# Attention in 11 parts per group of heads in place of 16, their transposes two parts behind, and two outputs earlier in the last group

## The chip, the cores and the metric

One core of a Trainium2 chip runs the kernel. A core has TensorE (PE, matmuls and transposes), VectorE (DVE), ScalarE (ACT) and GpSimd (POOL), which run their own instruction streams and wait for one another by semaphores; SyncE (SP) issues most DMAs. The metric is the time of one execution in microseconds: 1339.72 us, the median of 3 runs (1336.94 to 1344.49). The profile is of one further execution.

## The reference, cut to what matters

Four sequences of 512 tokens (width 256) go through a latent-attention layer, a mixture of experts, a state-space layer and a gated feed-forward layer. Only the attention is touched:

```python
q = rmsnorm(x @ w_qa, q_norm_w) @ w_qb            # 16 heads, 128 plain + 64 rotary columns
kv = rmsnorm(kv_c, kv_norm_w) @ w_kvb             # 64 latent columns, one rotary key for all heads
scores = jnp.einsum('blhd,bmhd->bhlm', q, k) * scale
scores = jnp.where(mask[None, None], scores, -1e30)        # causal
attn = jax.nn.softmax(scores, axis=-1)
out = jnp.einsum('blhm,bmhd->blhd', attn, v).reshape(B, L, H * DV) @ w_o
```

Everything is computed in float32 here; the causal mask is added by a small bf16 matmul.

## The kernel before, in words

**Rows and groups.** The attention takes one sequence at a time, called a row here (`b` from 0 to 3), and in it four groups of four heads (`hg` 0 to 3; `g` counts the 16 groups over all rows). The weights are folded so that a head's query is a 64-wide latent with a 64-wide rotary part, and its key and value are the shared latents: `QT` holds the turned queries of a group (two buffers), `KT` the keys, `V` the values.

**Parts.** A group is cut into `NU` = 16 parts `u` (one slot each), a tile of 128 queries `i = u // 4` by a head `h = u % 4`. Because of the causal mask part `u` has `(i + 1) * 128` score columns: 128 for the first four parts, then 256, 384 and 512. A part goes through: `scores` on PE (a float32 product, two matmul instructions, and the mask, L615 and L616) into one of three banks; `maximum` on DVE (L1001); `exps` on ACT (L829, which also gives the row sum); `inverse_sum` on DVE (L1006); `normalize` on DVE, in place in `prob` (L1012); `transposes` on PE, one per 128 columns, into one of two banks (L624); `evacuate` on DVE to the buffers `prob01`, `prob2`, `prob3` (L1021, L1024). Then `values` multiplies whole query tiles by `V` (L641; n = 0 takes tiles 0 and 1, n = 1 tile 2, n = 2 tile 3), and ACT copies the result to `OT` (`take_values`, L841). `output` (L712) multiplies a tile of `OT` by the folded output weights, eight products of 256 columns, and DVE adds it to `x` (`residual`, L950).

**The order of work** is written out by hand, per engine and slot `at`; an engine does its list in order. PE's slot: scores of part `at`; work for the next group's queries, if its slot says so (`rope_product` L542 and L546, `latent_product` L555 and L560, `rope_transposes` L567; in a row's last group the next row's `project`, L510); transposes of part `at - LAG`, with `LAG` = 3 (the last three parts of a group fall in the next group's first slots); values; routing products. DVE's slot: maximum of `at`, inverse sum of `at - 1`, evacuation of `at - LAG`, normalisation of `at - 1`, then a step of the routing of the row before (`route_slot`: the choice of six experts per token, L1226 to L1306). ACT's slot: the exponential of `at`, then copies (L795, L803, L809, L841). POOL turns queries (`rope`, L1125 to L1129) and sends the row before to the experts' buffer (`send`, L1375).

The slots of the extra work are in tables: `ROPES_AT` {1, 4}, `LATENTS_AT` 7, `TURN_AT` {11, 14}, `PROJECT_AT` {5, 9}, `VALUES_AT` {12: 0, 16: 1, 20: 2}, where a slot of 16 or more is `at - 16` in the next group. Semaphore counts keep the order: `exps` of part u needs the transposes of u - 4 (four `prob` buffers), scores of u the exponential of u - 3, transposes of u the evacuation of u - 2.

**Row ends.** After a row's last group the last transposes and values run, then the four outputs, mixed with the start of the next row. In row 3 outputs 0 and 1 stand in slots 14 and 15 of the last group; then values 1, the last transposes, values 2, a transposed half of the layer norm (L393), output 2, routing logits (L1183) and output 3. After that the shared expert (L1646 to L1665) runs beside the routing and sending of row 3, and then the experts' loop.

Of the kernel before, what the change touches and what calls it, by code (L numbers as in the profile page):

```python
# [15 lines left out]
P = 128  # L16
# [9 lines left out]
HG = 4  # L26
# [29 lines left out]
def build(nc, a, out):  # L56

    ctx = ExitStack()
    with ctx:
# [432 lines left out]
        def output_bank(b, i):  # L492
            return bank[(QUERY[0], QUERY[1], 4, 5)[i] if b == BATCH - 1 else 4 + i % 2]
# [7 lines left out]
        def att_tensor(pe):  # L501
# [48 lines left out]
            def latent_product(g, at):  # L550

                hg = g % GROUPS
                for p in range(2):
                    h = hg * HG + 2 * p
                    nc.tensor.matmul(bank[at[p]][:], wl1[:, h:h + 2, :].rearrange("p h c -> p (h c)"), cq1,  # L555
                                     start=True, stop=False)
                for c in range(0, SEQ, 2 * P):
                    for p in range(2):
                        r = slice(QL2 * p, QL2 * (p + 1))
                        last = nc.tensor.matmul(bank[at[p]][:, c:c + 2 * P], wl2[r, hg, :], cq2[r, c:c + 2 * P],  # L560
                                                start=False, stop=c + 2 * P == SEQ)
                last.then_inc(A["q"], 1)
# [23 lines left out]
            def first_latents(b):  # L586
                g = GROUPS * b
                pe.wait_ge(A["qs"], QSTEPS * g + 2)
                latent_product(g, (6, 7))
# [14 lines left out]
            def scores(g, u):  # L604
                i, h = u // HG, u % HG
                n = (i + 1) * P
# [3 lines left out]
                if h == 0 and i % 2 == 0:  # L610
                    pe.wait_ge(A["qte"], 2 * g + i // 2 + 1)
                if u == 0 and g % GROUPS == 0:
                    pe.wait_ge(A["kr"], g // GROUPS + 1)
                at = score_bank(g, u)
                nc.tensor.matmul(at[:, 0:n], QT[g % 2][:, h, i * P:(i + 1) * P], KT[:, 0:n], start=True, stop=False)  # L615
                nc.tensor.matmul(at[:, i * P:n], identb[:], futureb[:], start=False, stop=True)\  # L616
                    .then_inc(A["s"], 1)

            def transposes(g, u):
                i = u // HG  # L620
                pe.wait_ge(A["norm"], NU * g + u + 1)
                need(pe, A["pte"], NU * g + u - 1)
                for j in range(i + 1):
                    last = nc.tensor.transpose(bank[TRANS[u % 2]][:, j * P:(j + 1) * P],  # L624
                                               prob[:, u % 4, j * P:(j + 1) * P], ident)
                last.then_inc(A["pt"], 1)

            def values(g, n):
                tiles = VALUE_TILES[n]
                pe.wait_ge(A["pte"], NU * g + HG * (tiles[-1] + 1))  # L630
# [16 lines left out]
            def slot(g, at, with_next):  # L647
# [4 lines left out]
                elif not with_next:  # L652
# [1899 lines left out]
```

## Time and profile before

| | |
|---|---|
| median of 3 runs | 1339.72 us |
| the profiled execution's own time | 1341.87 us |
| its span, first to last instruction | 1340.0 us |
| mean granted clock of PE | 0.961 of full speed |
| busy in the span: PE, DVE, ACT, POOL | 90%, 61%, 36%, 28% |
| attention, from the first scores to the end of the last output | 59.5 to 638.2 us |
| the rest: before, and from there to the end | 59.5 us, 701.8 us |

The span is that of the profiled execution alone, and is compared with that execution's own time, not with the median. A share of busy time is an average over the whole program: PE's 90% doesn't say that PE sets the pace in each part of it. Where one engine waits for another is read from the stretches, the chain of waits and the timeline. Busy times of PE are modelled to each matmul's end and overlap; the time that a matmul takes of PE is the distance to the next one's start, which is what the chain of waits lists.

### The profile page before, as it was taken

The page shows a single profiled execution, that of the slowest core. Times are in us where ns is not written, and L with a number is a line of the kernel's source. Part 1 is how long each engine was busy: PE and PEld are TensorE (multiplying, and loading weights), DVE is VectorE, ACT ScalarE, POOL GpSimd, SP SyncE. Part 2 cuts the span into 40 slices and gives each one's busy share as a digit, 9 for nine tenths or more (in the row PEclk, how much of TensorE's full clock was granted, in tenths as well). Part 3 has the DMA queues.
Part 4 walks back from the last instruction along what each step waited for, and adds up shares of the span by engine and source line. Part 5 has one row for each costly group of instructions (what it writes and reads, how often), then busy time and mean ns, then how long its engine had stood idle before and what let it go on. Part 6 is the DMA issues. An engine that isn't in the chain of part 4 may idle for free.

```text
span 1340.0 us, 19647 instructions
## 1 busy us (share of the span) xinstructions
PE 1212.5 (90%) x6073; PEld 760.7 (57%) x6073; DVE 822.7 (61%) x2243; ACT 487.3 (36%) x1124; POOL 374.5 (28%) x462
## 2 busy tenths in 40 slices
PE   6899999999998899988979999998777959999988
PEld 3566566555655466555547777775434436465454
DVE  6477877788688777785433334336684655676431
ACT  2456435552555435552301111111522513525311
POOL 0242023251425423352520000213781450401200
PEclk9799999999999999999989999999888988999989
DMA  9999999999900100010458888872220020000000
GB/s 330 412 420 419 420 421 420 420 419 418 418 23 33 64 1 1 6 58 34 136 139 255 272 268 287 269 246 79 71 68 27 24 71 16 24 7 10 0 16 16
DMA packets 86624, 235.76 MB, mean 176 GB/s; under 512 B 9712, under 2 KB 20624, under 8 KB 86288
## 3 DMA queue, kind: packets, MB, share of 16 engines
q1 hardware_dynamic: 68112, 192.80, 38.8%
q0 software_dynamic: 9216, 25.18, 5.9%
q10 hardware_dynamic: 9216, 16.78, 3.3%
q8 instruction: 42, 0.69, 0.2%
q14 instruction: 38, 0.31, 0.1%
HBM read 66.96 MB, written 167.77 MB: 175 GB/s over the span
## 4 chain that ended last, share of the span: by engine, by line
PE 66%; DVE 21%; issue 5%; ACT 2%; another core or an unknown queue 2%; SPq 2%; DMA 1%; POOL 1%; ACTq 0%; POOLq 0%; DVEq 0%
PE bank L615 6%; PE bank L641 4%; PE bank L1505 4%; PE bank L624 4%; PE bank L1527 4%; PE bank L1766 3%; PE bank L1772 3%; DVE r L1012 3%; DVE negmax L1001 3%; PE bank L712 3%; PE bank L1783 3%; PE bank L542 2%; PE bank L1927 2%; PE bank L1490 2%
## 5 line engine op out<-in xcount | busy, mean ns | idle before, releaser
L829 ACT ACTIVATE r<-bank,negmax 128x128 f32<-128x128 f32 (+3 forms) x256 | 135.2, 528 | 179.7 <-DVE negmax L1001 172.3
L615 PE MATMUL bank<-r 128*128 128x512 f32 (+3 forms) x512 | 185.8, 446 | 2.9 <-ACT r L809 2.9
L1001 DVE TENSOR_REDUCE negmax<-bank 128x1 f32<-128x128 f32 (+3 forms) x256 | 123.9, 485 | 49.5 <-PE bank L616 37.0
L624 PE MATMUL bank<-tables,r 128*128 128x128 f32 x640 | 118.3, 284 | 24.8 <-DVE r L1012 22.5
L1125 POOL TENSOR_TENSOR r<-r,tables 128x256 f32<-128x256 f32 x56 | 40.9, 731 | 338.4 <-ACT r L795 333.0
L1375 POOL DMA_INDIRECT sent<-r,slots x96 | 93.6, 975 | 102.1 <-ACT r L829 52.2
L624 PEld LDWEIGHTS bank<-tables,r 128*128 128x128 f32 x640 | 70.3, 142 | 87.2 <-DVE r L1012 49.7
L1614 DVE COPY r<-bank 128x512 f32<-128x512 f32 x64 | 41.2, 686 | 116.2 <-PE bank L1536 75.0
L1012 DVE TENSOR_SCALAR r<-r,rrow 128x128 f32<-128x128 f32 (+3 forms) x256 | 112.1, 438 | 0.3
L615 PEld LDWEIGHTS bank<-r 128*128 128x128 f32 x512 | 79.2, 194 | 21.4 <-issue 16.8
L1021 DVE COPY late<-bank 128x256 f32<-128x256 f32 (+1 forms) x128 | 60.8, 475 | 29.5 <-PE bank L624 24.4
L1392 POOL DMA_INDIRECT r<-sent,slots x16 | 15.2, 953 | 213.2 <-DMA sent<-r 209.5
L1728 POOL TENSOR_TENSOR r<-tables,r 128x1024 f32<-128x1024 f32 x16 | 31.2, 1963 | 155.1 <-DVE r L2147 126.9
L1572 ACT ACTIVATE r<-bank 128x512 f32<-128x512 f32 x32 | 19.1, 598 | 145.8 <-PE bank L1505 138.6
L712 PE MATMUL bank<-spent,r 128*128 128x256 f32 x256 | 59.9, 390 | 3.9 <-ACT r L841 3.9
L1505 PE MATMUL bank<-r 128*128 128x256 f32 x256 | 62.5, 388 | 0.0
L1527 PE MATMUL bank<-r 128*128 128x256 f32 x256 | 61.3, 382 | 0.0
L712 PEld LDWEIGHTS bank<-spent,r 128*128 128x128 f32 x256 | 48.8, 195 | 14.2 <-ACT r L841 5.5
L1606 DVE COPY r<-bank 128x512 f32<-128x512 f32 x64 | 41.3, 684 | 24.4 <-PE bank L1490 22.4
L616 PE MATMUL bank<-futureb,identb 128*128 128x128 bf16 x256 | 56.2, 220 | 0.0
L1527 PEld LDWEIGHTS bank<-r 128*128 128x128 f32 x256 | 48.0, 190 | 8.9 <-issue 2.7
L1021 DVE COPY w2buf<-bank 128x512 f32<-128x512 f32 x64 | 43.2, 678 | 14.0 <-PE bank L624 14.0
(289 smaller groups left out, 2449.4 us busy)
## 6 DMA issues: line engine op xcount, KB each, us to landing
sent<-gath SPq DMA_DIRECT2D x8, 16384.0 KB, 93.7
r<-waT_dram SPq DMA_DIRECT2D x64, 304.0 KB, 3.1
r<-sent SPq DMA_DIRECT2D x64, 256.0 KB, 3.9
sent<-r ACTq DMA_DIRECT2D x64, 256.0 KB
w2buf<-wcT_dram SPq DMA_DIRECT2D x64, 48.0 KB, 3.2
r<-w_o_dram SPq DMA_DIRECT2D x1, 2048.0 KB, 22.5
sent<-gath SPq DMA_DIRECT2D x2, 1024.0 KB, 60.6
out_dram<-x SPq DMA_DIRECT2D x4, 512.0 KB, 2.9
```

The lines of the kernel that those rows point to most:

```text
L615: nc.tensor.matmul(at[:, 0:n], QT[g % 2][:, h, i * P:(i + 1) * P], KT[:, 0:n], start=True, stop=False)
L616: nc.tensor.matmul(at[:, i * P:n], identb[:], futureb[:], start=False, stop=True)\
L624: last = nc.tensor.transpose(bank[TRANS[u % 2]][:, j * P:(j + 1) * P], prob[:, u % 4, j * P:(j + 1) * P], ident)
L641: last = nc.tensor.matmul(bank[VALUE][KVL * half:KVL * (half + 1), c:c + 2 * P], V[:, j, :], p[:, 2 * half:2 * half + 2, :].rearrange("p h ...
L712: last = nc.tensor.matmul(output_bank(b, i)[:, 0:DIM], OT[:, c, i * P:(i + 1) * P], wvo[:, c, :], start=(c == 0), stop=(c == HEADS // 2 - 1))
L829: nc.scalar.activation(prob[:, u % 4, 0:(i + 1) * P], score_bank(g, u)[:, 0:(i + 1) * P], ACT.Exp, bias=negmax[:, u:u + 1], scale=1.0, acc ...
L1001: nc.vector.tensor_reduce(negmax[:, u:u + 1], score_bank(g, u)[:, 0:(i + 1) * P], axis=AX.X, op=ALU.max, negate=True).then_inc(A["max"], 1)
L1012: nc.vector.tensor_scalar(p, p, rrow[:, u:u + 1], None, ALU.mult).then_inc(A["norm"], 1)
L1021: nc.vector.tensor_copy(prob_at(i)[:, :, h, :], src.rearrange("p (j l) -> p j l", j=i + 1))\
L1375: nc.gpsimd.indirect_dma_start(sent[:, :], bass.IndirectOffsetOnAxis(ap=slots[:, t, k:k + 1], axis=0), xn1_first[:, n // TOPK, :] if c == ...
L1505: last = nc.tensor.matmul(bank[2][:, t * ROWS:(t + 1) * ROWS], wb[:, 2 * q + t, k * EI:k * EI + EA], tokens(q, t, k), start=(k == 0), stop ...
L1527: nc.tensor.matmul(to[t][:, half * DIM:(half + 1) * DIM], hid_a[:, q % 2, c:c + P], wb[:, 2 * q + t, KC * EI:KC * EI + DIM], start=(half = ...
```

## The change

1. **Parts.** `UNITS` lists 11 parts: the four heads of query tile 0 in one part, those of tile 1 in two parts of two heads, and one part for each head of tiles 2 and 3 as before. A joined part has 4 x 128 or 2 x 256 = 512 score columns in one bank. Its heads' products, masks and transposes stay single instructions, as do its exponentials (one per head); its maximum, reciprocal, normalisation and evacuation are one instruction each. The normalisation of a joined part is a `tensor_tensor` with the reciprocals broadcast, in place of `tensor_scalar`.
2. **LAG** is 2 in place of 3.
3. **Slots.** Ropes at 1 and 3, latents in halves of 256 columns at 5 and 6 (their copies at 7 and 8), turns at 9 and 10, projections at 3 and 6. Values 0 at slot 8, values 1 at 10, values 2 at slot 4 of the next group; in a row's last group values 0 at 6, values 1 at 10 and values 2 after the last transposes. Routing steps move to the fewer slots, `shares` and `portions` to slots 3 and 4 of group 2.
4. **Outputs.** In the last group of row 3 outputs 0 and 1 stand in slots 8 and 9, their residual and statistics on DVE in slots 9 and 10. Output 2 comes before values 2 and uses the bank of output 0.
5. **Sends.** The 16 sends in a row's last group wait for parts in proportion.

```diff
-        NU = HG * TB
-        LAG = 3
+        UNITS = [(0, range(HG)), (1, range(0, 2)), (1, range(2, HG))]
+        UNITS += [(i, range(h, h + 1)) for i in range(2, TB) for h in range(HG)]
+        NU = len(UNITS)
+        LAG = 2
-        ROPES_AT = {1: 0, 4: 1}
-        LATENTS_AT = 7
-        TURN_AT = {11: 0, 14: 1}
-        PROJECT_AT = {5: 0, 9: 1}
-        VALUES_AT = {12: 0, 16: 1, 20: 2}
+        ROPES_AT = {1: 0, 3: 1}
+        LATENTS_AT = {5: 0, 6: 1}
+        LATENTS_OUT = {7: 0, 8: 1}
+        TURN_AT = {9: 0, 10: 1}
+        PROJECT_AT = {3: 0, 6: 1}
+        OUTPUT_AT = {8: 0, 9: 1}
+        def values_at(g, at):
+            if g % GROUPS == GROUPS - 1:
+                return {6: 0, 10: 1, NU + LAG: 2}.get(at)
+            return {8: 0, 10: 1, NU + 4: 2}.get(at)
+        def unit(u):
+            i, hs = UNITS[u]
+            return i, hs, (i + 1) * P, slice(HG * i + hs[0], HG * i + hs[-1] + 1)
...
-                nc.tensor.matmul(at[:, 0:n], QT[g % 2][:, h, i * P:(i + 1) * P], KT[:, 0:n], start=True, stop=False)
-                nc.tensor.matmul(at[:, i * P:n], identb[:], futureb[:], start=False, stop=True)\
-                    .then_inc(A["s"], 1)
+                for m, h in enumerate(hs):
+                    nc.tensor.matmul(at[:, m * w:(m + 1) * w], QT[g % 2][:, h, i * P:(i + 1) * P], KT[:, 0:w],
+                                     start=(m == 0), stop=False)
+                for m, h in enumerate(hs):
+                    last = nc.tensor.matmul(at[:, m * w + i * P:(m + 1) * w], identb[:], futureb[:],
+                                            start=False, stop=(h == hs[-1]))
+                last.then_inc(A["s"], 1)
...
-                if g == BATCH * GROUPS - 1 and at in (NU - 2, NU - 1):
-                    output(BATCH - 1, at - NU + 2)
+                if g == BATCH * GROUPS - 1 and at in OUTPUT_AT:
+                    output(BATCH - 1, OUTPUT_AT[at])
...
-                slot(b * GROUPS + GROUPS - 1, NU + 4, False)
                 if not more:
                     norm_tensor_half(pe, N1, b, 0, xn1_first, 7)
                     output(b, 2)
+                slot(b * GROUPS + GROUPS - 1, NU + LAG, False)
+                if not more:
                     route_logits(pe, b, 7, HALVES[0], b)
                     output(b, 3)
...
+                for m in range(len(hs)):
+                    c, n = slice(m * w, (m + 1) * w), cols.start + m
+                    last = nc.scalar.activation(prob_of(g, u)[:, c], score_bank(g, u)[:, c], ACT.Exp,
+                                                bias=negmax[:, n:n + 1], scale=1.0, accum_out=rowsum[:, n:n + 1])
+                last.then_inc(A["exp"], 1)
...
-                nc.vector.tensor_scalar(p, p, rrow[:, u:u + 1], None, ALU.mult).then_inc(A["norm"], 1)
+                if len(hs) == 1:
+                    nc.vector.tensor_scalar(p, p, rrow[:, cols], None, ALU.mult).then_inc(A["norm"], 1)
+                else:
+                    p = p.rearrange("p (h n) -> p h n", h=len(hs))
+                    nc.vector.tensor_tensor(p, p, rrow[:, cols].unsqueeze(2).to_broadcast([P, len(hs), w]),
+                                            ALU.mult).then_inc(A["norm"], 1)
...
+                        if g == BATCH * GROUPS - 1 and at - 1 in OUTPUT_AT:
+                            residual(b, OUTPUT_AT[at - 1])
+                            stats_of(b, OUTPUT_AT[at - 1])
+                if b == BATCH - 1:
+                    norm_variance_half(dve, N1, b, 0)
                 for at in range(NU, NU + LAG):
                     slot(b * GROUPS + GROUPS - 1, at)
+                    if b == BATCH - 1 and at == NU:
+                        norm_apply_half(dve, N1, b, 0, xn1_first)
```

## Rows read from the trace of the kernel before

**Rows 1.** The page, part 1: busy us and share of the span.
```profile
PE 1212.5 (90%) x6073; PEld 760.7 (57%) x6073; DVE 822.7 (61%) x2243; ACT 487.3 (36%) x1124; POOL 374.5 (28%) x462
```
**Rows 2.** Stretches: us, busy by engine (instructions), PE's clock, DMA share, GB/s.
```profile
108.97:135.99 27.02, 26.84 (x167) 16.63 (x165) 20.50 (x65) 16.58 (x49) 9.18 (x16) 1.00 1.02 420
135.99:169.62 33.63, 32.56 (x186) 18.21 (x184) 27.16 (x76) 15.19 (x46) 0.00 (x0) 1.00 1.02 420
...
250.53:281.92 31.39, 29.32 (x166) 17.34 (x165) 25.36 (x88) 16.69 (x48) 17.36 (x24) 0.95 1.02 420
...
373.54:403.82 30.28, 28.56 (x171) 17.38 (x169) 23.78 (x80) 17.00 (x49) 9.18 (x16) 1.00 0.01 4
403.82:433.80 29.98, 27.48 (x166) 16.61 (x165) 24.45 (x87) 16.58 (x48) 17.34 (x24) 1.00 0.10 36
433.80:472.62 38.82, 33.85 (x186) 18.20 (x184) 31.82 (x112) 16.03 (x48) 15.62 (x16) 1.00 0.16 55
...
496.13:525.28 29.15, 26.85 (x150) 17.37 (x149) 20.82 (x80) 16.84 (x46) 9.23 (x16) 0.94 0.00 1
...
585.52:610.94 25.42, 19.85 (x124) 11.56 (x122) 19.83 (x85) 11.57 (x36) 12.71 (x13) 1.00 0.19 68
```
**Rows 3.** Chain of waits, rows 1 to 3: start, us on the chain, what.
```profile
226.58 0.69 DVE w2buf L1021
227.27 0.41 DVE r L1012
...
228.54 0.92 PE bank L542 x4
229.46 0.63 PE bank L546 x4
...
230.35 1.88 PE bank L641 x16
...
234.12 1.77 PE bank L555 x4
235.89 1.06 PE bank L560 x8
...
252.86 2.76 PE bank L641 x12
...
302.06 1.45 PE bank L641 x12
```
**Rows 4.** By form: instructions | busy us, mean ns | idle before.
```profile
L1001 DVE TENSOR_REDUCE negmax<-bank 128x1 f32<-128x512 f32 x64 | 44.1, 688 | 9.1 <-PE bank L616 4.4 <-remote 3.3
...
L1012 DVE TENSOR_SCALAR r<-r,rrow 128x512 f32<-128x512 f32 x64 | 30.9, 483 | 0.0
L1012 DVE TENSOR_SCALAR r<-r,rrow 128x128 f32<-128x128 f32 x64 | 27.7, 432 | 0.3
L829 ACT ACTIVATE r<-bank,negmax 128x128 f32<-128x128 f32 x64 | 23.5, 368 | 39.1 <-DVE negmax L1001 37.5 <-issue 1.2
L1306 DVE SCALAR_TENSOR_TENSOR scratch<-r,scratch 128x64 f32<-128x64 f32 x96 | 21.6, 280 | 0.1
L1125 DVE TENSOR_TENSOR r<-r,tables 128x256 f32<-128x256 f32 x8 | 6.6, 820 | 13.5 <-ACT r L795 13.3
L2207 DVE TENSOR_TENSOR r<-r 128x512 f32<-128x512 f32 x8 | 5.5, 692 | 0.3
```
**Rows 5.** Chain of waits at the end of row 3.
```profile
607.34 2.87 another core or an unknown queue
...
610.94 5.41 PE bank L712 x16
616.35 0.86 PE bank L615 x2
...
617.26 0.44 PE bank L624 x4
...
634.66 3.51 PE bank L712 x16
```

More of the change, by code:

```diff
@@ L548, in rope_product, with latent_product @@
                         .then_inc(A["q"], 1)
-            def latent_product(g, at):
-                hg = g % GROUPS
+            def latent_product(g, at, part):
+                hg, c = g % GROUPS, slice(part * 2 * P, (part + 1) * 2 * P)
                 for p in range(2):
                     h = hg * HG + 2 * p
-                    nc.tensor.matmul(bank[at[p]][:], wl1[:, h:h + 2, :].rearrange("p h c -> p (h c)"), cq1,
+                    nc.tensor.matmul(bank[at[p]][:, c], wl1[:, h:h + 2, :].rearrange("p h c -> p (h c)"), cq1[:, c],
                                      start=True, stop=False)
[L557 to L562, printed above, removed]
+                for p in range(2):
+                    r = slice(QL2 * p, QL2 * (p + 1))
+                    last = nc.tensor.matmul(bank[at[p]][:, c], wl2[r, hg, :], cq2[r, c], start=False, stop=True)
+                if part:
+                    last.then_inc(A["q"], 1)
             def rope_transposes(half, at):
@@ L588, in first_latents @@
                 pe.wait_ge(A["qs"], QSTEPS * g + 2)
-                latent_product(g, (6, 7))
+                for part in range(2):
+                    latent_product(g, (6, 7), part)
             def first_turned(b, half):
@@ L679, in slot @@
                     transposes(g - 1, u + NU)
-                if at in VALUES_AT:
-                    values(g, VALUES_AT[at])
-                elif at + NU in VALUES_AT and not first:
-                    values(g - 1, VALUES_AT[at + NU])
+                if values_at(g, at) is not None:
+                    values(g, values_at(g, at))
+                elif not first and values_at(g - 1, at + NU) is not None:
+                    values(g - 1, values_at(g - 1, at + NU))
                 if g >= GROUPS and not final:
                     route_slot(g // GROUPS - 1, g, at)
-                if g == BATCH * GROUPS - 1 and at in (NU - 2, NU - 1):
-                    output(BATCH - 1, at - NU + 2)
+                if g == BATCH * GROUPS - 1 and at in OUTPUT_AT:
+                    output(BATCH - 1, OUTPUT_AT[at])
             def route_slot(c, g, at):
@@ L990, in route_slot @@
                         route.farthest(c)
[L991 removed]
+                if hg == 2 and at == 3:
                     route.shares(c)
[L993 removed]
+                if hg == 2 and at == 4:
                     route.portions(c)
[L995 to L996 removed]
+                if hg >= 2 and at in (5, 7, 9):
+                    route.weigh(c, 3 * (hg - 2) + (at - 5) // 2)
@@ L1081, in att_vector @@
                 if not more:
-                    for i in HALVES[0]:
-                        residual(b, i)
-                        stats_of(b, i)
-                    norm_variance_half(dve, N1, b, 0)
-                    norm_apply_half(dve, N1, b, 0, xn1_first)
                     residual(b, 2)
@@ L1153, in att_pool @@
                     g = GROUPS * b + GROUPS - 1
-                    for u in range(NU):
-                        pool.wait_ge(A["exp"], NU * g + u + 1)
-                        send(b - 1, 2 * TB + u)
+                    for n_sent in range(HG * TB):
+                        pool.wait_ge(A["exp"], NU * g + n_sent * NU // (HG * TB) + 1)
+                        send(b - 1, 2 * TB + n_sent)
         R = {k: sem(f"r_{k}") for k in
```

138 lines of the change are left out of this document (71 added, 67 removed).

## The prediction

> **What bounds the kernel now.** The page's busy shares come first [rows 1]: PE 90%, DVE 61%, ACT 36%. No engine but PE can set the whole time. The 90% counts matmuls to their modelled ends, though, and hides gaps, so I read the stretches group by group [rows 2]. A middle group takes 27.02 us in row 0, where no routing runs. In row 2 groups 1 and 2 take 30.28 and 29.98, and row 3 repeats both within 0.02 us. The last group with the row's end takes 33.63 in row 0 and 38.82 in row 2.
>
> The third view, the chain of waits, gives what PE really spends, from start to start [rows 3, 5]: 512 score columns 0.86 us, four transposes 0.44, values 1.45 for 12 instructions and 1.88 for 16, ropes 0.92 + 0.63, latents 1.77 + 1.06, an output 3.5. A middle group's work is then 40 blocks of 128 columns at 0.215 (8.6), 16 masks at an estimated 0.06, half a transpose (0.9), 40 transposes (4.4), values 1.45 + 1.45 + 1.88 (4.8), two ropes (3.1), latents (2.8) and eight turning transposes (0.9): **25.5 us**. So PE stands idle 1.5 us per middle group in row 0 and, with 0.9 for the counts in group 1, 3.9 and 4.5 in row 2. Where it is idle, the chain runs over DVE (226.58: copy, then normalisation, then PE again) [rows 3]. The early parts with ropes, latents and values 1 and 2 are PE's, the parts of 384 and 512 columns DVE's. There DVE has, per part of 512, 0.69 + 0.69 + 0.48 and a reciprocal of about 0.1, with overlap some 1.7 us, and PE 0.86 + 0.06 + 0.44 = 1.4 [rows 3 to 5]. Routing adds to DVE: one `weigh` is four of 0.28 us with overlap, about 0.8.
>
> PE's clock belongs to this. Most stretches have 1.00; that of 250.53 has 0.95 and that of 496.13 has 0.94 [rows 2]. The 12-instruction values at 252.86 took 2.76 us and not the 1.45 of 302.06: the 1.2 GHz level in place of 2.4, after a gap at a group's edge. Each such drop costs about 1.3 us.
>
> Over the rows, PE's idle time in the attention is 7.6 us in row 0: 1.5 in each of three groups and 3.1 in the last. That last one is 33.63 less 30.5 of work: 18.7 of its own (25.5 without ropes, latents and turns), 4.6 carried over from the group before (12 transposes, values 1 and 2), and by their columns 5.3 for three projections and 1.9 for the squares' sums. The same way the last group of row 2 has 8.3. The first group of a later row has 23.5 of work (nothing carried over, 2.6 of norm transposes and routing logits) and in row 3 takes 29.15 us (the stretch from 496.13), idle 5.5 [rows 2]. That makes 22 us in rows 1 and 2 each, and 28 in row 3. That is all this change can touch: the PE work stays.
>
> **What the change does, part by part.**
>
> *Joined parts.* PE issues the same products, masks and transposes, plus the split of the latents, whose columns and 2.8 us are the same: 0 on PE. ACT still has 16 exponentials. DVE loses 20 instructions per group. For tiles 0 and 1 it had eight parts, by pitch about 0.8 us each for 128 columns and 1.05 for 256: 7.4 us. Now three parts of 0.69 + 0.1 + 0.68 + x. The trace has no such normalisation. The nearest rows are a `tensor_tensor` of 512 columns at 0.69 (below), and one of 256 columns beside POOL's ropes at 0.82, so up to about 1.2 for 512 (above) [rows 4]; the old form of 128 columns also averages 0.43 beside POOL. I take 0.7 to 0.9, near the plain row. Three parts are 6 us, saving about 1.5 us of DVE per group, in a stage where DVE was waiting: directly worth nothing.
> The Trainium skill (VectorE: DVE Perf Modes, the perf-mode tier table) speaks against this edit: float32 `tensor_scalar` runs at 2x, `tensor_tensor` at 1x only. The rows agree, 483 against 692 ns for 512 columns. By that rule one joined 512 costs 0.2 us more than one old 512, but it replaces two or four small ones.
>
> *The price of joining* is a longer serial chain at each group's start: scores 1.1, maximum 0.7, four exponentials at about 0.36 pitch 1.5 [rows 4], reciprocal 0.15, normalisation 0.7 to 0.9. That is 4.5 us with hand-overs. PE has in that time scores 0 to 2 (3.0), two carried transposes (0.9) and a rope (1.55), so it waits some 0.5 us at slot 2. It waits 0.7 more at slot 4, where the transposes of part 2 wait behind DVE's 0.68 copy and 0.7 normalisation. In a row's last group, with no rope, these become 1.2, and 0.8 once or twice. With POOL beside it add 0.5: **1.7 us of new idle per middle group**.
>
> *LAG 2.* PE now waits in slot `at` for the normalisation of `at - 2`, which DVE issues in slot `at - 1` behind the evacuation of `at - 2 - 1`. Queued behind PE's wait are the values and the next scores, for which DVE's maximum waits. The loop transposes, copy (0.46 to 0.6), normalisation (0.33 to 0.39), hand-overs is about 1.2 us beyond the transposes, against next scores of 0.7 to 0.92: up to 0.3 us in a slot without extra work. Nearly every slot of tiles 2 and 3 now has such work, and there the cost is nothing; that cover is missing in slots 5 and 7 to 9 of a row's last group.
>
> *Moved work* is the gain. Tiles 0 and 1 lose the second rope, the latents and values 1 and 2 (7.7 us); tiles 2 and 3 get them. There PE now has 19.5 us for eight parts against DVE's 12 and up to 3.7 of routing, so PE sets the pace where DVE did. What is late next is ACT (about 8.7 us of exponentials and copies in the four parts of tile 3, against PE's 9.0), just hidden. Two new waits: in group 0 values 0 stand behind `top`'s copy (0.3), in group 1 behind `ranks` (0.55). Group 2, with only `weigh` steps behind a normalisation, is covered by the values. POOL and SP: ropes start earlier, sends are the same 96 of about 1 us; POOL is no bound.
>
> **The sum**, as idle time of PE before and after:
> - Row 0: 7.6 before. After: 1.3, 1.7, 1.7 and 4.6 (no routing, so little to be won): 9.3. Loss 2, rounded up.
> - Rows 1 and 2: about 22 each before. After: group 0 3.0 (start chain, `apply_norm` before part 1's normalisation), group 1 3.7, group 2 2.2, last group 5.5 (1.2 + 0.8 + 0.8 at its start, about 2.2 where `weigh` meets slots 7 to 9 without cover, 0.5 at the end), one clock drop 1.3: 15.7. Gain 6 each.
> - Row 3, groups 0 to 2: 5.5 + 3.9 + 4.5 = 14 before, 8.9 and most of one drop after. Gain 4.
> - Row 3, last group: now 585.52 to 638.17 [rows 2, 5]: 52.65 us, 38.6 of it work (18.7 + 4.6 + four outputs 14.0 + 1.3 for norm transposes and logits). Output 0 waited for the copy of values 0, at the end of a 2.87 us hold of ACT, and ran at the lower clock in 5.41 in place of 3.5 [rows 5]. Placed at slots 8 and 9 the outputs (7.0 us) cover DVE's `weigh` and residual steps, and output 2 covers the last evacuation. Walking the slots, 42.7 us from first scores to last output, plus the 1.9 of values 1 and transposes that now stand before it: 44.6, gain 8. I keep 7.
>
> Gain: -2 + 6 + 6 + 4 + 7 = **21 us**. All after output 3 runs the same list and shifts whole. From the profiled execution's own 1341.87 (span 1340.0) that is 1320.9; the runs' median is 2.15 lower, so **1318.7**.
>
> **Rivals.**
> - *The slack was needed* (18%). For: my hand schedule has DVE and PE within 0.2 us of each other in most slots, and LAG 3 absorbed what is now a wait. Against: slots with extra PE work hide it. If each of the 16 groups loses 0.8 us more, 13 of the 21 go: 1332.
> - *PE-bound everywhere* (17%). For: about 7 us are lost to clock drops before, and short gaps may not trigger them; output 0's hold may go. Then the idle after is some 14 us less than I have: 1305.
> - *Slower: the joined chain at each group's start* (9%). Place: parts 0 to 2. Price: normalisations at 1.2 beside POOL, PE idle 3 us in a piece and then at 1.2 GHz, where PE runs 1.3 us longer. It decides from 1.3 us per group above my sum (21 / 16); at 1.9 it is 30 us: 1349. Against: PE has 5.5 us of its own in that time.
> - *The end gives it back* (8%). Routing of row 3 may wait on something that isn't earlier: the hold of 2.87 us has no owner in the view and may return elsewhere, and sends keep their order. Row 3's 7 us go, and 3 more: 1329.
> - My forecast 48%, own range 1311 to 1326.
> The Trainium skill (GPSIMD Engine Reference, Specifications) says that POOL shares SBUF interfaces with DVE instructions in a two-port mode or with two SBUF inputs. Here DVE's 256-column `tensor_tensor` took 0.82 us beside POOL while 512 columns alone took 0.69, which agrees; by that rule the joined form stays exposed as the old one was.
>
> Within 0.5% is 6.7 us, about what can be told from no change. Faster by more: my case, PE-bound, the returned end, most of the slack case: 0.81. Same: 0.10. Slower: 0.09. Range 1302 to 1337.
>
> **What would show it.** Right: middle groups of rows 1 to 3 near 28 us, group 2 gaining more than group 1, row 0's unchanged or up to 1 us longer; last output ending near 617; the stretch from there to the end still about 702 us; joined normalisation 0.7 to 0.9 us; PE waiting for it in slots 2 and 4. Wrong: idle PE before transposes in slots 5 to 10 of middle groups (slack), the clock at 0.95 in more stretches than before (chain), or row 3 ending as early without the total following.

## The result and the profile after

The changed kernel takes 1351.18 us in the median (14 runs, 1347.25 to 1357.14) against 1341.38 for the kernel before beside it: ratio **1.008**, interval 1.006 to 1.011. It is slower by about 11 us, where 21 us of gain were forecast; the time is outside the range. One execution of the kernel before took 6696.8 us and is left out of the ratio. Its profiled execution took 1347.26 us (span 1345.4).

The page of the changed kernel, part 1, answers to [rows 1]:

```profile
PE 1210.2 (90%) x6137; PEld 767.7 (57%) x6137; DVE 807.0 (60%) x1923; ACT 479.9 (36%) x1124; POOL 388.0 (29%) x462
```

DVE has 320 instructions less, PE works as long as before. Its stretches, from one group's first scores to the next one's, with the columns of [rows 2]:

```profile
113.78:143.03 29.25, 27.89 (x170) 17.38 (x168) 18.96 (x44) 16.22 (x49) 10.26 (x16) 1.00 1.02 420
...
354.76:384.16 29.40, 27.50 (x171) 18.23 (x169) 22.01 (x65) 17.96 (x51) 10.60 (x16) 1.00 0.52 212
384.16:415.57 31.41, 29.00 (x174) 18.28 (x172) 22.91 (x64) 16.40 (x50) 10.27 (x16) 1.00 0.00 1
415.57:445.59 30.02, 27.95 (x171) 17.38 (x169) 23.67 (x73) 15.87 (x47) 18.16 (x24) 1.00 0.10 36
445.59:483.04 37.45, 31.45 (x170) 17.21 (x168) 27.73 (x77) 14.36 (x46) 15.53 (x16) 1.00 0.16 57
...
597.73:646.09 48.36, 40.86 (x232) 29.54 (x231) 28.77 (x97) 16.23 (x46) 15.48 (x16) 0.96 0.13 44
646.09:1345.40 699.31, 628.36 (x2881) 394.96 (x2880) 354.53 (x754) 181.35 (x291) 171.65 (x158) 0.95 0.35 110
```

A middle group of row 0 went from 27.02 to 29.25 us; group 1 of row 2 from 30.28 to 31.41; group 2 stayed (29.98, 30.02); the last group of row 2 gained 1.4, that of row 3 with its outputs 4.3 (52.65 to 48.36). From the first scores to the last output's end the attention is 587.4 us in place of 578.6; of these 8.8, row 0 alone has 9.3 up to its first output. The rest after the last output is 699.3 (701.8 before): nothing comes back there. The granted clock is 1.00 in all stretches of the attention but the last (0.96), where the kernel before has 0.95 and 0.94 in two of those shown [rows 2]: this execution has fewer clock drops and is slower all the same. Where row 0's middle group lost its time is in the chain of waits of the changed kernel (start, us, what), slots 1 to 4:

```profile
117.50 0.63 PE bank L568 x4
118.14 0.60 PE bank L651 x4
...
118.76 0.69 DVE w2buf L1065
119.45 0.71 DVE r L1047
...
120.21 0.66 PE bank L651 x4
...
123.74 0.69 DVE late L1065
124.44 0.61 DVE r L1047
...
125.09 0.66 PE bank L651 x4
```

PE has done a rope and the transposes of two parts ago (118.14). DVE's evacuation of those (L1065) and then the normalisation (L1047) stand between them and the next transposes. The timeline of PE says how much of that PE could not fill (start, us, form, idle before it):

```profile
119.42 0.27 PE L640 MATMUL bank<-futureb,identb 128*128 128x128 bf16 x2
120.21 0.66 PE L651 MATMUL bank<-tables,r 128*128 128x128 f32 x4 [0.51 <-DVE r L1047]
...
124.19 0.22 PE L640 MATMUL bank<-futureb,identb 128*128 128x128 bf16 x1
125.09 0.66 PE L651 MATMUL bank<-tables,r 128*128 128x128 f32 x4 [0.68 <-DVE r L1047]
```

0.51 and 0.68 us, and 0.22 more for each of these transposes, which take 0.66 on the chain after a wait and 0.44 without one [rows 5].

### The profile page after: what moved, and what is told of

Read it like the earlier page. It is cut to its first block, busy times and chain, and to the rows that moved or that the text cites. A ratio compares the mean times of both kernels' runs of the same rounds, so it can differ in the third digit from the quotient of the medians.

```text
span 1345.4 us, 19287 instructions
## 1 busy us (share of the span) xinstructions
PE 1210.2 (90%) x6137; PEld 767.7 (57%) x6137; DVE 807.0 (60%) x1923; ACT 479.9 (36%) x1124; POOL 388.0 (29%) x462
## 4 chain that ended last, share of the span: by engine, by line
PE 65%; DVE 18%; SPq 5%; issue 5%; another core or an unknown queue 2%; ACT 2%; DMA 1%; POOL 1%; ACTq 0%; POOLq 0%; DVEq 0%
PE bank L637 6%; PE bank L651 6%; PE bank L668 5%; PE bank L1809 3%; PE bank L1815 3%; PE bank L739 3%; PE bank L1826 3%; PE bank L1570 2%; PE bank L1548 2%; PE bank L1860 2%; PE bank L577 2%; PE bank L1970 2%; PE bank L564 2%; DVE late L1065 2%
## 5 line engine op out<-in xcount | busy, mean ns | idle before, releaser
L637 PE MATMUL bank<-r 128*128 128x512 f32 (+3 forms) x512 | 172.2, 443 | 2.8 <-ACT r L837 2.8
L1030 DVE TENSOR_REDUCE negmax<-bank 128x1 f32<-128x384 f32 (+3 forms) x176 | 112.3, 638 | 71.3 <-PE bank L640 63.7
L651 PE MATMUL bank<-tables,r 128*128 128x128 f32 x640 | 106.4, 285 | 44.3 <-DVE r L1044 21.9
L1168 POOL TENSOR_TENSOR r<-r,tables 128x256 f32<-128x256 f32 x56 | 46.3, 827 | 340.0 <-ACT r L823 334.2
L1065 DVE COPY late<-bank 128x384 f32<-128x384 f32 (+1 forms) x112 | 67.9, 607 | 45.6 <-PE bank L651 41.6
L637 PEld LDWEIGHTS bank<-r 128*128 128x128 f32 x512 | 76.2, 190 | 21.7 <-issue 14.0
L1615 ACT ACTIVATE r<-bank 128x512 f32<-128x512 f32 x32 | 19.1, 597 | 145.1 <-PE bank L1548 135.5
L1044 DVE TENSOR_SCALAR r<-r,rrow 128x384 f32<-128x384 f32 (+1 forms) x128 | 57.5, 450 | 0.0
L739 PEld LDWEIGHTS bank<-spent,r 128*128 128x128 f32 x256 | 48.4, 193 | 11.3 <-ACT r L871 2.8
L1065 DVE COPY w2buf<-bank 128x512 f32<-128x512 f32 x64 | 43.8, 684 | 15.8 <-PE bank L651 14.6
L1570 PEld LDWEIGHTS bank<-r 128*128 128x128 f32 x256 | 48.0, 190 | 8.9 <-issue 2.7
L859 ACT ACTIVATION_READ_ACCUMULATOR r<-bank,negmax 128x1 f32 x256 | 50.4, 197 | 0.0
```

Source lines behind the costliest of these rows:

```text
L637: nc.tensor.matmul(at[:, m * w:(m + 1) * w], QT[g % 2][:, h, i * P:(i + 1) * P], KT[:, 0:w], start=(m == 0), stop=False)
L651: last = nc.tensor.transpose(turned_bank(g, u)[:, c:c + P], prob_of(g, u)[:, m * w + j * P:m * w + (j + 1) * P], ident)
L739: last = nc.tensor.matmul(output_bank(b, i)[:, 0:DIM], OT[:, c, i * P:(i + 1) * P], wvo[:, c, :], start=(c == 0), stop=(c == HEADS // 2 - 1))
L859: last = nc.scalar.activation(prob_of(g, u)[:, c], score_bank(g, u)[:, c], ACT.Exp, bias=negmax[:, n:n + 1], scale=1.0, accum_out=rowsum[: ...
L1030: nc.vector.tensor_reduce(negmax[:, cols], score_bank(g, u)[:, 0:len(hs) * w] .rearrange("p (h n) -> p h n", h=len(hs)), axis=AX.X, op=ALU ...
L1044: nc.vector.tensor_scalar(p, p, rrow[:, cols], None, ALU.mult).then_inc(A["norm"], 1)
```

## The experiments

My theory after the result (**L**): LAG 2 is the loss; the transposes of a part wait for its own normalisation, queued behind the last evacuation. Against it: the latents' split, the `weigh` steps beside POOL, the joining itself. The sets ran on several chips, which differ (the kernel before: 1297 to 1343 us), so each number stands against the kernel before of its own set.

### LAG 3

```diff
-        LAG = 2
+        LAG = 3
```

> The changed kernel with one edit: LAG is 3 again, so the transposes of a part stand three slots behind its scores; parts, slots of the other work and outputs stay changed. Theory L (the shorter lag took PE's cover away: in the changed kernel PE waits 0.5 us before the transposes of part 0, 0.7 before those of part 2, and in a row's last group DVE and PE take turns): the waits in slots 2 and 4 go, the middle groups of row 0 fall from 29.25 to about 28 us, the last groups by 2 to 3 us, together 1.5 us in each of 16 groups, about 24 us: ratio to the kernel before about 0.99. Rival J (the serial chain of a joined part is the cost whatever the lag): the same waits return one slot later, total within 4 us of the changed kernel, ratio 1.005 to 1.011. Rival M (moved work: values and latents in places where PE has none to spare) says the same as J for the total but with no waits at slots 2 to 4.

1326.54 us against 1342.96: ratio 0.990 (0.986 to 0.994). The whole loss turns into a gain. Stretches of this kernel, those of the table above:

```profile
112.15:139.16 27.01, 27.01 (x171) 17.37 (x169) 19.38 (x44) 16.16 (x49) 10.39 (x16) 1.00 1.02 419
...
342.67:370.37 27.70, 26.81 (x166) 17.80 (x165) 22.16 (x65) 17.85 (x51) 10.11 (x16) 1.00 0.98 401
370.37:399.90 29.53, 27.94 (x174) 18.27 (x172) 22.93 (x62) 16.27 (x48) 10.40 (x16) 1.00 0.02 7
399.90:427.71 27.81, 27.51 (x170) 17.39 (x169) 24.68 (x74) 15.60 (x49) 18.64 (x24) 1.00 0.11 39
427.71:466.01 38.30, 32.18 (x172) 18.18 (x172) 28.21 (x78) 14.61 (x46) 15.84 (x16) 0.96 0.16 56
...
574.96:617.60 42.64, 39.04 (x234) 28.53 (x235) 29.21 (x98) 16.54 (x46) 16.37 (x16) 1.00 0.14 50
```

Row 0's middle group is PE from end to end: 27.01 us, all busy. The same slots in its chain:

```profile
115.87 0.63 PE bank L568 x4
116.51 0.59 PE bank L651 x4
117.09 0.86 PE bank L637 x4
...
118.07 0.44 PE bank L651 x4
...
132.66 1.45 PE bank L668 x12
134.10 1.06 PE bank L637 x2
```

So the waits of slots 2 and 4 are LAG's price and not that of the joined parts, whose chain is as long here (DVE's copy and normalisation still take 0.69 and 0.79 us, while PE works). From one part's first scores to the next one's, in a middle group of row 0, slot 2 is 0.7 us shorter than in the changed kernel and slot 4 0.9; the slots of tiles 2 and 3 give the other 0.6 of the 2.24. In rows 1 to 3 slots 2 and 4 differ by the same in groups 1 and 2 (0.7 and 0.9), so most of LAG's price lies there, at a group's start and not in tiles 2 and 3.

### The latents' product whole, at LAG 2

```diff
+                if part:
+                    return
-                    nc.tensor.matmul(bank[at[p]][:, c], wl1[...], cq1[:, c], ...)
+                    nc.tensor.matmul(bank[at[p]][:], wl1[...], cq1, ...)
```

> The changed kernel with one edit: the latent product is issued whole in slot 5 (four instructions of 512 columns, eight of 256) and not in halves in slots 5 and 6. In the changed kernel a half takes 1.64 us of PE (0.92 + 0.63 and a start), two 3.28, where the whole took 2.93 before. All theories: 0.35 us less in each of 12 groups plus 4 first ones, about 5 us, if PE sets the pace there: ratio about 1.004. If slot 6 now runs into DVE instead, the gain is under 2 us.

1353.17: ratio 1.009 (1.006 to 1.013), no gain where about 5 us were expected; row 0's middle groups 29.34. What PE saves, it then waits.

### The kernel before with LAG 2

```diff
-        LAG = 3
+        LAG = 2
```

> The kernel before with one edit: LAG is 2 in place of 3, with 16 separate parts and the old slots. Theory L: loses by itself, above all in the stage of 384 and 512 columns where DVE sets the pace and at group ends, 0.7 to 1 us a group, 11 to 16 us: ratio 1.008 to 1.012. Rival J: lag 2 alone costs under 4 us, ratio within 0.997 to 1.003, since separate parts have short chains.

1416.08: ratio **1.056** (1.052 to 1.060), 73 us and not 11 to 16. A middle group of row 0 takes 32.54, one of later rows 34 to 35.5. With separate parts of tile 1 the loop (transposes, copy, normalisation) takes 1.21 us, from 125.97 to 127.18, and the next scores with their mask only 0.49 (0.43 and 0.06 on the chain). Its chain in tiles 0 and 1:

```profile
125.97 0.34 PE bank L624
...
126.33 0.29 DVE late L1024
126.63 0.51 DVE r L1012
...
127.18 0.33 PE bank L624
```

L is right in kind; I under-priced it again. The parts and the places that came with LAG 2 win back most of what it costs.

### POOL turns all four tiles before it sends

```diff
-                        if b and hg == GROUPS - 1 and i % 2:
-                            ...
-                            for m in range(4):
-                                send(b - 1, 2 * (i - 1) + m)
+                    if b and hg == GROUPS - 1:
+                        send_ready(pool, b - 1)
+                        for m in range(8):
+                            send(b - 1, m)
```

> The changed kernel with one edit: in group 2 of rows 1 to 3 POOL turns all four query tiles of the next group before its eight sends, in place of four sends between the second and third tile. In the changed kernel the weigh step of slot 5 (four scalar_tensor_tensor of 64 columns) runs beside POOL's turning products and takes 1.96 us in place of 0.83, and PE waits for the next normalisation. Theory C (that contention costs): group 2 of rows 1 to 3 shortens by 1.0 to 1.5 us each, 3 to 4.5 us in all, ratio about 1.005. Rival: the joined normalisations now meet the turns instead, or PE has other waits there, under 1 us.

1363.59: ratio 1.017 (1.013 to 1.021), slower: group 2 of row 2 takes 33.4 and not 30.0. The contention is real in the changed kernel, where the `weigh` step of slot 5 takes 2.03 us (its timeline):

```profile
433.15 0.73 POOL L1172 TENSOR_TENSOR r<-r 128x256 f32<-128x256 f32 x1
433.22 0.74 DVE L1349 SCALAR_TENSOR_TENSOR scratch<-r,scratch 128x64 f32<-128x64 f32 x1
...
433.89 0.28 DVE L1349 SCALAR_TENSOR_TENSOR scratch<-r,scratch 128x64 f32<-128x64 f32 x1
```

The edit does what it was meant to: here the step takes 0.89 us. But the sends, now at the end of the group, brought something worse, a standstill of ACT and DVE (below), so the total says nothing of what the contention cost:

```profile
450.04 0.65 ACT L871 COPY r<-bank 128x256 f32<-128x256 f32 x2 [2.79 <-remote]
450.10 0.69 DVE L1030 TENSOR_REDUCE negmax<-bank 128x1 f32<-128x512 f32 x1 [3.79 <-PE bank L640]
```

### LAG 3 with whole latents; with later outputs; with unmoved work; with other slots in the last groups

These four ran together; the kernel before took 1299.62. LAG 3 alone was not in this set.

> LAG 3 and the latents' product whole in slot 5, the rest as changed. With LAG 3 row 0's middle groups were PE from end to end (27.0 us). If the split costs PE its 0.36 us per group (3.29 against 2.93) and that is exposed where PE never waits, this is 12 x 0.36 = 4 us faster than LAG 3 alone: ratio to before 0.987, row 0's middle groups 26.65. Rival: at slot 5 one piece of 2.9 us puts DVE's and ACT's parts late by as much as it saves, as it did at LAG 2: ratio 0.990, middle groups 27.0 or more.

Edit: the latents as above. 1273.65, ratio 0.978 (0.975 to 0.981); row 0's middle groups 26.59: the 0.4 us per group is real once PE never waits.

```diff
-        OUTPUT_AT = {8: 0, 9: 1}
+        OUTPUT_AT = {9: 0, 10: 1}
...
+                    residual(b, 1)
+                    stats_of(b, 1)
```

> LAG 3, and in the last group of row 3 outputs 0 and 1 in slots 9 and 10, one slot later than in the change (the last two parts, where the kernel before has them). If placing the outputs earlier is what shortened that group, by covering DVE's weigh steps and statistics, this takes 2 to 4 us longer than LAG 3 alone: ratio 0.992 to 0.993, from the last group's first scores to the end of the last output 45 in place of 42.6. Rival: the place matters little, because PE has the same work left at the end; the gain came from output 2 before values 2: ratio 0.990.

1278.83, ratio 0.982 (0.979 to 0.985); the last group with its outputs takes 41.0 us. With slots 8 and 9 it takes 40.6 in the kernel with whole latents and 41.9 in that with other slots, both of this set. The 2 to 4 us that were expected of the later slots aren't there.

```diff
-        ROPES_AT = {1: 0, 3: 1}
-        LATENTS_AT = {5: 0, 6: 1}
-        TURN_AT = {9: 0, 10: 1}
-            return {8: 0, 10: 1, NU + 4: 2}.get(at)
+        ROPES_AT = {0: 0, 1: 1}
+        LATENTS_AT = {4: 0}
+        TURN_AT = {7: 0, 9: 1}
+            return {7: 0, NU: 1, NU + 3: 2}.get(at)
```

> LAG 3 and joined parts, but ropes, latents (whole), turns and values where they stood by time before the change: ropes in slots 0 and 1, latents in 4, turns in 7 and 9, values 0 in 7, values 1 and 2 in slots 0 and 3 of the next group. It prices the moving. If moving PE's extra work from tiles 0 and 1 to tiles 2 and 3 is what gains (my sum's reason), most of the 13.5 us go: ratio 0.996 to 1.003, PE waiting in slots 7 to 10. Rival: joining gains by itself, since it takes twenty instructions per group off DVE, and the moving is worth little: ratio 0.988 to 0.992.

1301.44, ratio 1.000 (0.999 to 1.002). The latents are whole here too, so its twin is the first kernel of this set, 1273.65: moving the work is worth 28 us at LAG 3. Group 1 of row 2, this kernel and then its twin:

```profile
373.78:406.55 32.77, 29.45 (x170) 18.33 (x169) 21.62 (x61) 16.15 (x49) 10.34 (x16) 0.95 0.01 3
363.68:392.99 29.31, 27.52 (x170) 17.68 (x168) 22.70 (x62) 16.24 (x48) 10.38 (x16) 1.00 0.21 87
```

Joining and the new outputs without the move give nothing together. That isn't a clean price of joining: row 3's last group takes 42.1 us here and 52.65 in the kernel before, while row 0's middle groups take 27.6 in place of 27.0 and group 1 of row 2 32.8 in place of 30.3. So the gain of the outputs hides a loss elsewhere.

```diff
-        PROJECT_AT = {3: 0, 6: 1}
+        PROJECT_AT = {3: 0, 8: 1}
-                if hg >= 2 and at in (5, 7, 9):
-                    route.weigh(c, 3 * (hg - 2) + (at - 5) // 2)
+                if hg == 2 and at in (5, 7, 9):
+                    route.weigh(c, (at - 5) // 2)
+                if hg == 3 and at in (1, 3, 5):
+                    route.weigh(c, 3 + (at - 1) // 2)
```

> LAG 3, and in a row's last group the three weigh steps in slots 1, 3, 5 in place of 5, 7, 9 and the second projection in slot 8 in place of 6. At LAG 3 PE waits in slots 8 to 10 there for DVE (1.5 us per part in row 0; with weigh 0.9 more in two of them), while it never waits in slots 2 to 7. So this should give back 1.5 us in row 0 (the projection fills a wait) and 2 to 3 us in each of rows 1 and 2, 1 to 2 in row 3: ratio 0.984 to 0.986. Rival: the waits only move to slots 3 to 6, or the stretch in which ACT and DVE stand still beside the sends (2 to 5 us in each of these groups) covers them: ratio 0.989 or more.

1272.75, ratio 0.978 (0.975 to 0.981): a row's last group goes from 33.55 us (the kernel with later outputs) to 31.9 in row 2, but in row 0, where 1.5 us were expected too, only from 31.70 to 31.55.

### LAG 3 and the changed kernel side by side, and both edits together

> The kernel with LAG 3 once more, beside the changed kernel itself, because the last set of four ran where the kernel before took 1299.6 us in place of 1343, without the 2 to 5 us in which ACT and DVE stood still in each last group beside POOL's sends. If LAG is worth the same everywhere, its ratio is 0.980 to 0.990 and it is 22 to 26 us faster than the changed kernel. Rival: part of LAG 3's gain was luck with those standstills; then it is under 18 us faster than the changed kernel where they are missing.

1329.62 against 1341.03: 0.990 (0.987 to 0.993).

> The changed kernel itself, beside its variants. If the loss at LAG 2 is a loop of DVE and PE and nothing else, its ratio is 1.008 where the standstills are there, and 0.998 to 1.004 where they are missing, with middle groups of row 0 at 29.25 us in either case. Rival: it depends on the run of the sends; then the middle groups change.

1355.39: 1.011 (1.006 to 1.016). So LAG 3 is worth 26 us in this set, the one in which the two kernels ran side by side.

> LAG 3, latents' product whole in slot 5, weigh steps of the last group in slots 1, 3, 5 and the second projection in slot 8: both earlier edits together. If both gains are of different places (0.36 us in each of 12 groups; 1.7 us in each last group), they add: about 8 us under LAG 3 alone, ratio 0.972 to 0.984 by where it runs. Rival: they overlap, and it is within 3 us of the better one.

1316.89: 0.983 (0.978 to 0.988), 12.7 us under LAG 3 alone where 8 were expected. In a later set, against a kernel before of 1301.82, the same kernel took 1272.13: 0.978 (0.976 to 0.981), which is no better than either edit alone on such a chip (0.978 and 0.978). So whether the two gains add isn't shown; the standstills below differ from run to run and stand in the 12.7. It beats the kernel before in both sets.

### LAG 3, work moved, parts separate

```diff
-        UNITS = [(0, range(HG)), (1, range(0, 2)), (1, range(2, HG))]
-        UNITS += [(i, range(h, h + 1)) for i in range(2, TB) for h in range(HG)]
+        UNITS = [(i, range(h, h + 1)) for i in range(TB) for h in range(HG)]
```

with the tables' slots shifted by five.

> LAG 3 and all of PE's extra work, routing steps and outputs at the changed kernel's places in time, but sixteen separate parts as before (ropes in slots 4 and 8, latents in 10 and 11, turns in 14 and 15, values in 13, 15 and slot 9 of the next group). It prices joining where the work is moved. If joining is needed for the move, since eight small parts cost DVE 7.4 us and three joined ones 6, and PE has now nothing beside them, this is 10 to 25 us slower than LAG 3 joined: PE waits in the first eight slots of each group. Rival: joining is worth nothing by itself, LAG 3 covers small parts too: within 5 us of it.

1361.20, ratio 1.016 (1.011 to 1.021): 32 us over LAG 3 with joined parts of the same set. A middle group of row 0 loses only 1.0 us (28.00), group 0 of later rows 7 (34.7 against 27.7). Its chain there:

```profile
368.29 0.27 PE bank L650
...
368.80 0.79 DVE r L1045
369.59 2.61 DVE r L343 x4
372.20 0.33 DVE negmax L1031
```

`apply_norm` (L343, 2.61 us) stands on DVE among small parts, and three of them ahead don't cover it. Of the 29.5 us that this kernel's attention takes longer than at LAG 3 with joined parts, 22 lie in group 0 of rows 1 to 3, where `apply_norm` runs, here in slot 4. The kernel before, with separate parts and PE's extra work in the early slots, has it in slot 1 and takes 27.4 to 29.2 us for that group. Another slot for `apply_norm` wasn't tried, so how much of the 32 us is the price of separate parts stays open; where no routing runs it is 1.0 us a group.

### The sends after values 0, and the standstill

On most chips ACT's copy of values 0 in a last group, and mostly DVE's next instruction with it, starts 2 to 5 us after PE's work for it has ended. In the kernel before ACT and DVE both wait in row 3 (2.87 on the chain) [rows 5], and DVE alone, 3.5 us, in rows 1 and 2. In the changed kernel ACT waits 3.7, 3.7 and 5.0 us in rows 1 to 3 (4.44 on the chain in row 3). In the kernel with both edits, beside a kernel before of 1341.03:

```profile
291.07 0.37 ACT L874 COPY r<-bank 128x256 f32<-128x256 f32 x1 [3.30 <-remote]
291.13 0.56 DVE L1035 TENSOR_REDUCE negmax<-bank 128x1 f32<-128x384 f32 x1 [3.56 <-remote]
```

```diff
+                        if n_sent == 0:
+                            pool.wait_ge(A["ote"], 3 * g + 1)
```

> The same kernel, but in each last group POOL's 16 sends wait until ACT has copied values 0 (slot 6), where before they began with the group's first parts. The question is what the 2 to 5 us are in which ACT (its copy of values 0) and DVE (its next maximum) stand still together in each last group of rows 1 to 3, though PE's work for them has ended. If POOL's sends in flight hold them up, the copy of values 0 comes right after its product in all three rows, and the standstill goes (6 to 9 us faster) or moves behind slot 6, beside the sends (same time). Rival: it belongs to the place in the program and not to the sends; then ACT's copy of values 0 comes as late as before, with no send running.

1270.93 beside 1272.13 without the edit, where no trace shows a standstill: nothing to tell apart. A repeat (1270.32, against 1296.97) fell on such a chip too. The third run did not:

> The kernel with the last groups' sends after values 0, once more for the standstills. Where they are present: by the sends in flight, ACT's copy of values 0 follows its product within 0.5 us in all three last groups. Rival: it is late by 2 us or more with no send running. Where they are missing again the question stays open.

1328.81 against 1335.15, ratio 0.996 (0.993 to 0.998). The copy of values 0 now comes at once, and ACT and DVE stand still later, when the sends run (timeline of row 1's last group):

```profile
291.36 0.64 ACT L874 COPY r<-bank 128x256 f32<-128x256 f32 x2
...
302.55 0.96 POOL L1425 DMA_INDIRECT sent<-r,slots  x1 [0.30 <-issue]
303.55 0.37 ACT L874 COPY r<-bank 128x256 f32<-128x256 f32 x1 [4.53 <-remote]
303.81 0.96 POOL L1425 DMA_INDIRECT sent<-r,slots  x1 [0.30 <-issue]
304.98 0.69 DVE L1070 COPY w2buf<-bank 128x512 f32<-128x512 f32 x1 [5.65 <-remote]
```

It goes where the sends go, and is longer: LAG 3 alone, in the same set, took 1314.05. By what way sends delay ACT and DVE stays open. It isn't a rule either: the kernel before with LAG 2 ran on a chip that had them, and its trace shows none above 1.5 us. Nor are the standstills what makes one chip 42 us slower than another. After the last output, where no edit reaches, the traces take 669 to 672 us on the chips without them and 697 to 706 on the others, some 30 of the 42; why stays open.

### The changed kernel and LAG 3 a third time

> The changed kernel once more. Where the standstills are missing (the kernel before at about 1300 us): if the change's loss is the loop at LAG 2 alone, it stays within 0.6% of the kernel before (0.998 to 1.006), with row 0's middle groups at 29.25. If the standstills caused the loss, it is 0.985 or less there. Where they are present: 1.008 to 1.011, as in the two sets before.

1316.10 against 1296.97, no standstills: ratio **1.014** (1.011 to 1.017), with row 0's middle groups at 29.25. The standstills are not the loss; without them the changed kernel stands worse, and outside the 0.998 to 1.006 that I expected. The last group of rows 1 and 2 takes 36.5 us here and 37.5 to 40.7 in the changed kernel's two traces with standstills; at LAG 3 these are 33.55 and 38.2 to 41.9. So where they are missing the changed kernel wins 1 to 4 us per such group and LAG 3 5 to 8.

> LAG 3 alone once more. Where the standstills are missing (the kernel before at about 1300 us): 1275 to 1280, ratio 0.980 to 0.985, which is 35 us or more under the changed kernel there, against 25 us where they are present. Rival: LAG is worth 25 us everywhere, ratio about 0.994. Where they are present: 0.990 as in both earlier sets.

It ran where they are present: 1314.05 against 1335.15, 0.984 (0.980 to 0.988), better than the 0.990 expected there. For a chip without them there is only the kernel with later outputs, 20.8 us under its kernel before, where the changed kernel is 19.1 over its own. That puts LAG 3 at about 40 us there, across two chips and with one more edit.

## Why the prediction was wrong

**The step that failed in the sum** is the idle time before: "So PE stands idle 1.5 us per middle group in row 0", "22 us in rows 1 and 2 each, and 28 in row 3". PE's idle time by row, span less PE's busy time, from a row's first scores to the next row's (row 3: to its last output's end), in us:

| row | before, forecast | before, measured | after, forecast | after, measured | LAG 3, measured |
|---|---|---|---|---|---|
| 0 | 7.6 | 2.1 | 9.3 | 8.2 | 1.6 |
| 1 | 22 | 10.5 | 15.7 | 13.5 | 9.7 |
| 2 | 22 | 12.0 | 15.7 | 12.9 | 9.4 |
| 3 | 28 | 15.8 | 17 (28 less 4 and 7) | 13.9 | 6.4 |
| sum | 80 | 40.4 | 58 | 48.4 | 27.1 |

The time after was forecast within 10 us in 58; the time before was put at twice what it was, so the gain of 21 was taken from idle time that wasn't there. (The column counts work at the lower clock as busy. There are five such drops in the attention before, 1.3 us each by my price, and one after; they don't close the gap of 39.) The error sits in **PE's work in a middle group**, 25.5 us. The kernel with LAG 3 and whole latents runs such a group in 26.59 without a gap. So the kernel before had about 0.4 us of idle there, and not 1.5, and 1.7 in place of 1.5 looked like no loss. What my sum lacked are the turns from one kind of work to another: transposes after a rope take 0.59 and not 0.44, scores after values 1.06 and not 0.86 (the chain at LAG 3), seven times in a group. I had the right number before me: PE busy 26.84 of 27.02 us [rows 2], which I set aside as counted to modelled ends. The idle time before was added up from spans less work, and the one after from waits found, so the missing turns stood in the first and not in the second.

***LAG 2*, the step that failed in the mechanism**: "Nearly every slot of tiles 2 and 3 now has such work, and there the cost is nothing". The shorter lag is why the kernel is slower: LAG 3 is 26 us faster in the set that had both, 1.6 us for each of 16 groups, and about 40 by the comparison across chips without standstills. Of the 2.24 us that it takes in a middle group of row 0, tiles 2 and 3 have 0.6. The larger part, 1.6, is in slots 2 and 4, and I had walked into both waits, "some 0.5 us at slot 2" and "0.7 more at slot 4" (measured 0.51 and 0.68). But I booked them as the price of joining, where LAG 3 shows them to be gone. They were in the sum, and so LAG's price alone doesn't explain the error of 32 us; the idle time before does for the most part. My rival of the slack had the mechanism and 0.8 us per group. At the measured 1.6 it gives 1318.7 + 26 = 1345, against 1351.

**The signs that I named.** PE waits in slots 2 and 4, the joined normalisation takes 0.71 us and the rest behind the last output 699 us: as named. The groups 1 and 2 of rows 1 to 3 take 30.0 to 31.4 us and not 28; group 1 of row 2 loses 1.1 and group 2, which was to gain most, gains nothing; and the last output ends at 646.1 and not near 617. Of the signs of being wrong, the clock has fewer drops and not more, and idle time in slots 5 to 10 is the smaller part. The waits that cost most, those of slots 2 and 4, stood in my list of what would be right.

**The latents' split at no cost** was wrong by 0.4 us per group (1.55 us for each half against 2.83 for the whole, and one turn more), visible only where PE sets the pace: 27.01 against 26.59, of one set.

**Joined parts.** "0.7 to 0.9" for the joined normalisation holds: x48, mean 711 ns. Worth nothing directly: not refuted, but not shown either, since the kernel without the move (ratio 1.000) has the new outputs too. Separate parts with the move lost 32 us, which I had not seen; most of it is in group 0, with `apply_norm`.

**Moved work** as the gain was right: 28 us at LAG 3. With LAG 3 the kernel gains 16.4, 11.4 and 21.1 us in three sets, near the 21 forecast for LAG 2, but that is partly luck. By rows, in the profiled execution, it gains -1.4, 3.6, 4.3 and 14.4, where -2, 6, 6 and 11 were forecast, and from an idle time before of half the size.

**Row 3's last group.** 7 forecast, 4.3 measured at LAG 2 (10 at LAG 3). The 2.87 us hold returned as 4.44, as the fourth rival feared, and output 2 ran at the lower clock:

```profile
608.72 4.44 another core or an unknown queue
...
633.44 0.97 PE bank L651 x4
...
635.26 4.40 PE bank L739 x16
...
642.58 3.51 PE bank L739 x16
```

The 16 products took 4.40 us soon after a wait for the last normalisations, and 3.51 after PE had worked without a gap. The granted clock of the last stretch is 0.96, part of it the 1.2 GHz level.

**The joined chain** as a slower case named the way and, with 1349, nearly the time, but by chance: with the same chain at LAG 3 row 0's middle groups have no idle time, and the clock dropped less often and not more. **PE-bound everywhere** is refuted for LAG 2, and is what LAG 3 brings in row 0. Its drops of the clock did go in this execution (five before, one after), and the kernel was slower in spite of them. On `weigh` beside POOL's ropes the Trainium skill (GPSIMD Engine Reference, Specifications) says that POOL shares SBUF interfaces with DVE instructions that read two SBUF inputs. The trace agrees: one 128 x 64 instruction of the step took 0.74 us beside a POOL product and 0.28 otherwise, so slot 5 in group 2 was a poor place. At LAG 2 it is part of why group 2, which I had as the winner, gained nothing: slot 7 there is 1.0 us longer than at LAG 3, 0.3 in row 0, where no `weigh` runs. At LAG 3 the same step takes 2.44 us and the group 27.81, all but 0.3 of it PE's work: the contention is there and costs nothing.

## What to carry to other kernels

Price the slack first: run the loop that a shorter lag closes (evacuate, normalise, hand over) against what PE has in each slot, small slots first, and take the lag away as an edit by itself. Hold a hand sum of an engine's work against the busy time of the same stretch, and where they differ by more than the gain per stage, believe neither until the gap is named. Don't take one side of a difference from spans and the other from waits walked: what the hand sum lacks then counts as gain. Joining small parts and moving work onto large ones were tried apart here, at LAG 3: one alone gave nothing and the other lost.

## What the runs showed of the hardware

- Beside POOL's indirect sends ACT, DVE or both stood still for 2 to 7.7 us at a time, on some chips, and where the sends were moved it moved with them. Where the kernel before takes about 1300 us no trace shows it. In the same slots, row 2's last group took 38.30 us with it (granted clock 0.96) and 33.55 without. The cause is open.
- After a wait, four transposes take 0.66 us on the chain and 0.44 in a run; after a rope product 0.59. Such turns make 1 us of a group of 27.
